# Expert stage of a gated transformer block on one core: gate and up matmuls with the weights held in the array and 128 tokens passing

## The chip, the core and the metric

The kernel runs on one core of a Trainium2 chip. The metric is device time in microseconds (us) of one launch. A core has TensorE (PE: matmuls, which read SBUF and write PSUM, and whose weight loads the trace lists apart as PEld), VectorE (DVE), ScalarE (ACT), GpSimd (POOL) and SyncE (SP, here a DMA queue). The engines run their own instruction lists in order and meet at semaphores.

## The reference

The block does `x = x + tanh(g) * attention(layernorm(x), ctx)` and then a mixture of experts on 128 sequences of 128 tokens, 256 channels. What the change touches is the second part, cut to what matters:

```
x = x + jnp.tanh(g_ffn[0]) * _L0_ffn_ref(_layernorm(x, axis=-1), w_router, w_fc, w_gate, w_proj)

cap = int(LOAD * K * max(1, T / E))        # 16 slots per expert and sequence, K = 2, E = 16
gg = jnp.einsum('enc,ech->enh', expert_inputs, w_gate)
h  = jnp.einsum('enc,ech->enh', expert_inputs, w_fc)
h  = jax.nn.silu(gg) * h                   # h: 128 hidden channels
o  = jnp.einsum('enh,ehc->enc', h, w_proj)
y  = sum over the two chosen experts of probability * o
```

## The kernel before

Three blocks follow each other: `attention_block`, `routing_block` and `expert_block`. The change lies in the last one, but for one factor in `routing_block` (L983).

**Precision.** Every matmul of the expert block is split: each operand is a head (`_hi`, rounded to fp32r) and a rest (`_lo`), and `split_matmul` (L1256) issues three fp32r matmuls, head by head, head by rest and rest by head, each with a weight load of its own. The trace names a product as `out<-moving,stationary`.

**Units.** A unit is one step of a software pipeline written by hand. Unit n means two things at once: sequence n for the sequence-wise steps, and for the expert-wise steps the pair of experts j = n mod 8 in the group of eight sequences n div 8 (16 slots of each of 8 sequences are 128 token rows). The constants of L1046 say by how many units each step runs behind or ahead of GATE. In one turn of the loop each engine does, in this order:

- PE (L1263): OUTPUT of unit u-3, that is `EO`: 2 experts x 3 matmuls, 256 columns passing. HIDDEN of u-2: two transposes `HT` of the hidden tile. GATE of u, `GU`: 2 experts x 2 halves of the channels x 3 matmuls; here the tokens (`s_hi`, `s_lo`) are the stationary operand and 256 weight columns pass (128 of the gate, 128 of fc), so that a result has tokens on the partitions. DISPATCH of u+9, `DS`: 4 matmuls of 256 columns that pick a sequence's tokens into expert slots.
- ACT (L1169): copies `EO` to SBUF (`eo`), makes `h_hi` from the transposes, issues the DMA of `eo` to DRAM, makes `x_hi`, the tanh of the gate (`th`, L1195) and `s_hi`.
- DVE (L1208): `h_lo`, `pick`, the first half of the output sum (L1228), `(tanh+1)*gate` (L1235), times fc (`hid`, L1239), the second half of the output sum (L1243), `s_lo` (L1249). Silu is thus made of tanh, and the factor 0.5 sits in `weight` (L983).
- POOL (L1146): two indirect DMAs that gather a sequence's rows of `eo_d` (`first`, `second`, L1153; their descriptors are made on POOL), and `x_lo` (L1162).
- SP (L1122): the output's DMA, the load of `xn2_d` into a ring of 3 and of `x1_d` into a ring of 3.

The steps FETCH and COLLECT (gather and output sum) start only with unit 12 and 14, since a gather needs all experts of its group. PE runs 16 units of the 128 as the body of a loop; the other engines' lists are written out. The steps before the first GATE are nine units of DISPATCH alone.

Of the kernel before, what the change touches and what calls it, by code (L numbers as in the profile page):

```python
# [858 lines left out]
def routing_block(nc, ctx, T, D):  # L859
# [82 lines left out]
    def _(dve):  # L942
# [40 lines left out]
        then(dve.tensor_scalar(weight[:], prob[:], gates[:, 3:4], 0.5, ALU.mult, ALU.mult))  # L983
# [59 lines left out]
def expert_block(nc, ctx, T, D):  # L1043


    LOAD, PICK, DISPATCH, GATE, HIDDEN, OUTPUT, FETCH, COLLECT = -13, -11, -9, 0, 2, 3, 12, 14  # L1046
# [8 lines left out]
    def pb(name):  # L1055
# [4 lines left out]
    x_in_sb, xr, y_sb = tiles[:, 0:3], tiles[:, 3:6], tiles[:, 6:8]  # L1060
    x_hi = sb("x_hi", [P, 2, DIM], F32R)
# [4 lines left out]
    th = sb("th", [P, 2, 2, HID])  # L1066
    hid = sb("hid", [P, 2, 2, HID])
# [11 lines left out]
    names = ("x_hi_done x_lo_done pick_done ds_done s_hi_done s_lo_done gu_done th_done "  # L1079
             "gated_done hid_done ht_done h_hi_done h_lo_done eo_done eo_copied y_part_done out_done").split()  # L1080
    M = {n: sem(n) for n in names}
    x_in = [sem(f"xn2_in{r}") for r in range(3)]
    rows_in = [sem(f"rows_in{r}") for r in range(3)]
    x1_in = [sem(f"x1_in{r}") for r in range(3)]
    eo_out = [sem(f"eo_out{r}") for r in range(3)]
    y_out = [sem("y_out0"), sem("y_out1")]
    DS = [pb("DS0"), pb("DS1")]
    HT = [pb("HT0"), pb("HT1")]
# [24 lines left out]
    def flat(a):  # L1113
        return a.rearrange("p a b -> p (a b)")
# [5 lines left out]
    @block.sync  # L1120
    def _(sp):
        def step(unit, on):  # L1122
            n = unit(COLLECT)
            if on(COLLECT):
                sp.wait_ge(M["out_done"], n.n + 1)
                sp.dma_start(D["out"][bass.ds(n.n, 1)].rearrange("b t c -> t b c"),
                             y_sb[:, n.slot(2):n.slot(2) + 1]).then_inc(y_out[n.slot(2)], 16)
            n = unit(LOAD)
            if on(LOAD):
                wait_for(sp, M["x_hi_done"], n.n - 2)  # L1130
                wait_for(sp, M["x_lo_done"], n.n - 2)
                sp.dma_start(x_in_sb[:, n.turn(3):n.turn(3) + 1], D["xn2_d"][:, bass.ds(n.n, 1)]) \  # L1132
                    .then_inc(x_in[n.turn(3)], 16)
            n = unit(FETCH)
            if on(FETCH):
                wait_for(sp, M["y_part_done"], n.n - 2)
                sp.dma_start(xr[:, n.turn(3):n.turn(3) + 1], D["x1_d"][:, bass.ds(n.n, 1)]) \  # L1137
                    .then_inc(x1_in[n.turn(3)], 16)

        run_flat(sp, step)  # L1140
        for q in y_out:
            sp.wait_ge(q, 16 * (SEQS // 2))

    @block.gpsimd
    def _(pool):
        def step(unit, on):  # L1146
# [21 lines left out]
    def _(act):  # L1168
        def step(unit, on):  # L1169
            n = unit(OUTPUT)  # L1170
# [4 lines left out]
            n = unit(HIDDEN)  # L1175
            if on(HIDDEN):
                act.wait_ge(M["ht_done"], n.n + 1)
                wait_for(act, M["eo_done"], n.n - 1)
                act.activation(flat(h_hi[:, n.slot(2)]), HT[n.slot(2)][:, 0:2 * P], ACT.Copy) \
                    .then_inc(M["h_hi_done"], 1)  # L1180
# [5 lines left out]
            n = unit(PICK)  # L1186
            if on(PICK):
                act.wait_ge(x_in[n.turn(3)], n.landed(3))
                wait_for(act, M["ds_done"], n.n - 1)
                act.activation(x_hi[:, n.slot(2)], x_in_sb[:, n.turn(3)], ACT.Copy).then_inc(M["x_hi_done"], 1)  # L1190
# [191 lines left out]
```

## Time and profile before

| | us |
|---|---|
| median of 3 runs | 1836.87 (1833.91 to 1838.42) |
| the profiled execution's own time | 1835.99 |
| its span on the core | 1834.2 |
| PE / PEld busy | 1520.0 / 1222.3 |
| DVE / ACT / POOL busy | 1410.9 / 1133.7 / 1088.1 |
| expert stage, from the first DS matmul (1344.28 us) to the end | 489.9 |

An instruction's duration in the trace includes its latency, so neighbours on one engine overlap: what one more matmul costs is read from the distance of starts, not from its duration. "idle before" in brackets is time in which the engine stood still before that row, and what ended it; "issue" is a release that the profile doesn't name. PEclk is the granted TensorE clock, 1.00 for 2.4 GHz and 0.50 for 1.2 GHz.

### The profile page before, as it was taken

Reading aid. Unit: us, or ns where it says so; the run is one execution under the profiler, and the core shown is the slowest. Engines: PE = TensorE matmul, PEld = TensorE weight load, DVE = VectorE, ACT = ScalarE, POOL = GpSimd, SP = SyncE. Lnnn points to the kernel's source line nnn. Section 1 sums busy time; section 2 is a strip of 40 time slices with the busy share of each in tenths; the row PEclk is TensorE's granted clock in tenths of the full one; section 3 lists DMA queues with packets and bytes.
Section 4 is the critical chain, followed back from the end, with each engine's and each line's share of the span. In section 5 each row is a group of like instructions: output and inputs, shape, how many; then the busy total and the mean of one; then the engine's idle time right before and its main releaser. Section 6 shows DMA issues by size and latency. Waiting matters only on the chain. (4 is left out here: it accounts for less than half of the span.)

```text
span 1834.2 us, 50716 instructions
## 1 busy us (share of the span) xinstructions
PE 1520.0 (83%) x16843; PEld 1222.3 (67%) x16844; DVE 1410.9 (77%) x2993; ACT 1133.7 (62%) x2321; POOL 1088.1 (59%) x1490
## 2 busy tenths in 40 slices
PE   4888889988899898898988989986169888898871
PEld 3666666666666666666666666664059888898871
DVE  3777787777877777777777777775968999999964
ACT  3667667677666766766766767674236555565540
POOL 3455465555655555555555555551826888788866
PEclk9999999999999999999999999997569999999995
DMA  2112122121221211212212122242026888898876
GB/s 90 48 58 86 57 71 72 57 86 57 69 74 57 85 58 57 86 57 73 70 57 86 57 70 73 70 145 81 6 72 198 260 263 261 262 286 269 263 228 207
DMA packets 156096, 210.21 MB, mean 115 GB/s; under 512 B 18688, under 2 KB 104832, under 8 KB 156032
## 3 DMA queue, kind: packets, MB, share of 16 engines
q1 hardware_dynamic: 125312, 142.36, 24.5%
q0 software_dynamic: 12288, 33.57, 6.4%
q10 hardware_dynamic: 18432, 33.56, 5.1%
q8 instruction: 24, 0.39, 0.1%
q14 instruction: 40, 0.33, 0.1%
HBM read 125.54 MB, written 83.89 MB: 114 GB/s over the span
## 5 line engine op out<-in xcount | busy, mean ns | idle before, releaser
L505 DVE TRANSPOSE_TENSOR_REDUCE part_max<-ST 128x16 f32<-128x512 f32 x512 | 321.3, 685 | 171.9 <-PE ST L684 168.4
L360 ACT ACTIVATE probs_t<-ST 128x512 f32<-128x512 f32 x512 | 262.5, 596 | 68.2 <-PE ST L699 68.2
L711 PE MATMUL PO<-probs_t,v_aug 128*32 128x128 f32 x4096 | 205.2, 298 | 108.6 <-ACT probs_t L360 95.0
L288 POOL TENSOR_TENSOR ct_lo<-c_in_sb,ct_hi 128x512 fp32r<-128x512 f32 x64 | 82.4, 1288 | 278.0 <-ACT ct_hi L378 278.0
L711 PEld LDWEIGHTS PO<-probs_t,v_aug 128*32 128x32 f32 x4096 | 94.4, 114 | 204.5 <-ACT probs_t L360 192.6
L437 ACT ACTIVATE xn<-x_in_sb,off,rstd 128x256 f32<-128x256 f32 x128 | 70.0, 594 | 224.7 <-POOL off L284 224.7
L1190 ACT ACTIVATE x_hi<-scaled 128x256 fp32r<-128x256 f32 x128 | 53.5, 418 | 210.9 <-DMA scaled<-xn_d 131.9
L1259 PE MATMUL GU<-we_hi,s_hi 128*128 128x256 f32 x512 | 155.8, 304 | 0.0
L1153 POOL DMA_INDIRECT first<-eo_d,collect_row x128 | 126.0, 984 | 44.4 <-issue 24.0
L316 POOL TENSOR_TENSOR q_rest<-q_rot,q_head 128x512 f32<-128x512 f32 x64 | 82.4, 1288 | 112.7 <-ACT q_head L413 112.7
L1153 POOL DMA_INDIRECT second<-eo_d,collect_row x128 | 122.6, 958 | 42.3 <-issue 38.7
L1260 PE MATMUL GU<-we_hi,s_lo 128*128 128x256 f32 x512 | 145.2, 284 | 0.0
L1261 PE MATMUL GU<-we_lo,s_hi 128*128 128x256 f32 x512 | 145.1, 283 | 0.0
L1162 POOL TENSOR_TENSOR x_lo<-scaled,x_hi 128x256 fp32r<-128x256 f32 x128 | 115.2, 900 | 48.8 <-ACT x_hi L1190 46.7
L1259 PE MATMUL EO<-we_hi,h_hi 128*128 128x256 f32 x256 | 82.5, 322 | 53.2 <-issue 39.4
L366 ACT ACTIVATE out_t<-PO 128x512 f32<-128x512 f32 x128 | 78.6, 614 | 71.0 <-PE PO L711 71.0
L729 PE MATMUL F<-ident_sb,xn 128*128 128x128 f32 x512 | 91.8, 306 | 31.6 <-ACT xn L437 19.7
L679 PE MATMUL ST<-q_hi,k_hi 32*128 32x256 f32 x1024 | 94.6, 358 | 5.9 <-issue 5.4
L1260 PEld LDWEIGHTS GU<-we_hi,s_lo 128*128 128x128 f32 x512 | 98.6, 192 | 0.0
L1261 PEld LDWEIGHTS GU<-we_lo,s_hi 128*128 128x128 f32 x512 | 98.1, 192 | 0.0
L1259 PEld LDWEIGHTS GU<-we_hi,s_hi 128*128 128x128 f32 x512 | 97.9, 191 | 0.2 <-issue 0.2
L1259 PEld LDWEIGHTS EO<-we_hi,h_hi 128*128 128x128 f32 x256 | 49.0, 191 | 72.9 <-issue 63.2
(158 smaller groups left out, 5565.7 us busy)
## 6 DMA issues: line engine op xcount, KB each, us to landing
eo_d<-eo ACTq DMA_DIRECT2D x128, 256.0 KB
x_in_sb<-x SPq DMA_DIRECT2D x64, 256.0 KB, 2.8
c_in_sb<-ctx_t SPq DMA_DIRECT2D x64, 256.0 KB, 2.8
xr_sb<-x SPq DMA_DIRECT2D x64, 256.0 KB, 4.0
x_d<-x SPq DMA_DIRECT2D x64, 256.0 KB, 4.1
xn_d<-xn SPq DMA_DIRECT2D x64, 256.0 KB, 4.2
scaled<-xn_d SPq DMA_DIRECT2D x128, 128.0 KB
scaled<-x_d SPq DMA_DIRECT2D x128, 128.0 KB
```

The source lines that it names most:

```text
L288: pool.tensor_tensor(ct_lo[:].rearrange("p k b t -> p (k b t)"), c_in_sb[:, n.par].rearrange("p k b t -> p (k b t)"), ct_hi[:].rearrange(" ...
L316: pool.tensor_tensor(q_rest[:].rearrange("p k t -> p (k t)"), q_rot[:].rearrange("p k t -> p (k t)"), q_head[:].rearrange("p k t -> p (k t ...
L360: act.activation(probs_t[:, b, i].rearrange("p j q -> p (j q)"), ST[i][:], ACT.Exp) \
L505: dve.tensor_reduce(part_max[:, i, 0], ST[i][:].rearrange("p (c l) -> p c l", l=32), AX_X, ALU.max, apply_transpose=True).then_inc(M["part ...
L679: pe.matmul(ST[i][:, m * 2 * SEQ:(m + 1) * 2 * SEQ], k_part[rows, n.par, m, b], q_part[rows, n.par, m, b].rearrange("p e t -> p (e t)"), s ...
L711: last = pe.matmul(PO[32 * j:32 * j + 32, i * SEQ:(i + 1) * SEQ], v_aug[:, n.par, b, head], probs_t[:, b, i, j], start=True, stop=True)
L729: last = pe.transpose(F[:, (2 * k + b) * SEQ:(2 * k + b + 1) * SEQ], src[:, b, k * P:(k + 1) * P], ident[:])
L1153: pool.indirect_dma_start(out=dst[:, n.turn(3)], out_offset=None, in_=D["eo_d"][n.group].rearrange("r e c -> (r e) c"), in_offset=bass.Ind ...
L1162: pool.tensor_tensor(x_lo[:, n.slot(2)], x_in_sb[:, n.turn(3)], x_hi[:, n.slot(2)].bitcast(F32), ALU.subtract).then_inc(M["x_lo_done"], 1)
L1259: pe.matmul(out, lh, rh, start=first, stop=False)
L1260: pe.matmul(out, ll, rh, start=False, stop=False)
L1261: return pe.matmul(out, lh, rl, start=False, stop=last)
```

## The change

- GU: the weights become the stationary operand, 128 columns of one expert's gate or fc at a time (`part` 0 to 3), and the 128 token slots pass. 4 parts x 2 halves x 3 = 24 matmuls of 128 columns take the place of 12 of 256. The result has the hidden channels on the partitions, as EO's stationary operand needs them, and the two transposes HT with their PSUM banks go.
- ACT computes Silu itself (`gate`), and DVE multiplies by fc in one instruction in place of two. `h_hi` and `h_lo` are made from `gate` in SBUF. The factor 0.5 in `weight` goes.
- `x_lo` moves from POOL to DVE; its ring stays 2 deep, `x_hi` becomes 4 deep and its ACT step (HEAD) runs a unit earlier, its load 3 units ahead of it.
- The output is summed in place in the ring `xr`, which becomes 4 deep, and `y_sb` goes. SP's list is turned to load, fetch, output.
- HIDDEN and OUTPUT run one unit earlier (1 and 2 behind GATE).

```diff
-        then(dve.tensor_scalar(weight[:], prob[:], gates[:, 3:4], 0.5, ALU.mult, ALU.mult))
+        then(dve.tensor_scalar(weight[:], prob[:], gates[:, 3:4], None, ALU.mult))
...
-    LOAD, PICK, DISPATCH, GATE, HIDDEN, OUTPUT, FETCH, COLLECT = -13, -11, -9, 0, 2, 3, 12, 14
+    LOAD, HEAD, PICK, DISPATCH, GATE, HIDDEN, OUTPUT, FETCH, COLLECT = -14, -11, -10, -9, 0, 1, 2, 12, 14
...
-    x_in_sb, xr, y_sb = tiles[:, 0:3], tiles[:, 3:6], tiles[:, 6:8]
-    x_hi = sb("x_hi", [P, 2, DIM], F32R)
+    x_in_sb, xr = tiles[:, 0:4], tiles[:, 4:8]
+    x_hi = sb("x_hi", [P, 4, DIM], F32R)
...
-    th = sb("th", [P, 2, 2, HID])
-    hid = sb("hid", [P, 2, 2, HID])
+    gate = sb("gate", [P, 2, 2, HID])
...
-            n = unit(PICK)
-            if on(PICK):
-                pool.wait_ge(M["x_hi_done"], n.n + 1)
-                wait_for(pool, M["ds_done"], n.n - 1)
-                pool.tensor_tensor(x_lo[:, n.slot(2)], x_in_sb[:, n.turn(3)], x_hi[:, n.slot(2)].bitcast(F32),
-                                   ALU.subtract).then_inc(M["x_lo_done"], 1)
...
+            n = unit(HIDDEN)
+            if on(HIDDEN):
+                act.wait_ge(M["hid_done"], n.n + 1)
+                wait_for(act, M["eo_done"], n.n - 1)
+                act.activation(flat(h_hi[:, n.slot(2)]), flat(gate[:, n.slot(2)]), ACT.Copy) \
+                    .then_inc(M["h_hi_done"], 1)
...
-                wait_for(act, M["hid_done"], n.n - 1)
-                act.activation(th[:, n.slot(2)], GU[n.slot(2)][:].rearrange("p (e f n) -> p e f n", e=2, f=2)[:, :, 0],
-                               ACT.Tanh, scale=0.5).then_inc(M["th_done"], 1)
+                wait_for(act, M["h_lo_done"], n.n - 1)
+                act.activation(gate[:, n.slot(2)], GU[n.slot(2)][:].rearrange("p (e f n) -> p e f n", e=2, f=2)[:, :, 0],
+                               ACT.Silu).then_inc(M["gate_done"], 1)
...
             n = unit(PICK)
             if on(PICK):
+                dve.wait_ge(M["x_hi_done"], n.n + 1)
                 wait_for(dve, M["ds_done"], n.n - 1)
+                dve.tensor_tensor(x_lo[:, n.slot(2)], x_in_sb[:, n.turn(4)], x_hi[:, n.turn(4)].bitcast(F32),
+                                  ALU.subtract).then_inc(M["x_lo_done"], 1)
...
+            n = unit(GATE)
+            if on(GATE):
+                gu = GU[n.slot(2)][:].rearrange("p (e f n) -> p e f n", e=2, f=2)
+                dve.wait_ge(M["gate_done"], n.n + 1)
+                dve.tensor_tensor(gate[:, n.slot(2)], gate[:, n.slot(2)], gu[:, :, 1], ALU.mult).then_inc(M["hid_done"], 1)
...
-                dve.scalar_tensor_tensor(out=th[:, n.slot(2)], in0=th[:, n.slot(2)], scalar=1.0, in1=gu[:, :, 0],
-                                         op0=ALU.add, op1=ALU.mult).then_inc(M["gated_done"], 1)
...
-                for e in range(2):
-                    last = pe.transpose(HT[n.slot(2)][:, e * P:(e + 1) * P], hid[:, n.slot(2), e], ident[:])
-                last.then_inc(M["ht_done"], 1)
...
-                for e in range(2):
-                    at = n.j * (4 * HID) + e * 2 * HID
+                for part in range(4):
+                    at = n.j * (4 * HID) + part * HID
                     for k in range(KC):
-                        last = split_matmul(GU[n.slot(2)][:, e * 2 * HID:(e + 1) * 2 * HID],
-                                            [t[:, n.side, k, n.j * 2 + e].rearrange("p b s -> p (b s)")
-                                             for t in (s_hi, s_lo)],
-                                            [w[:, k, at:at + 2 * HID] for w in w_gu], k == 0, k == KC - 1)
+                        last = split_matmul(GU[n.slot(2)][:, part * P:(part + 1) * P],
+                                            [w[:, k, at:at + HID] for w in w_gu],
+                                            [t[:, n.side, k, n.j * 2 + part // 2].rearrange("p b s -> p (b s)")
+                                             for t in (s_hi, s_lo)], k == 0, k == KC - 1)
```

Two engines' lists show the move. PE, in the loop body, from the end of one unit's EO into its GU, before:

```order
L1261 MATMUL EO<-we_lo,h_hi 128x256
L1280 MATMUL HT<-ident,hid 128x128 x2
L1259 MATMUL GU<-we_hi,s_hi 128x256
L1260 MATMUL GU<-we_hi,s_lo 128x256
L1261 MATMUL GU<-we_lo,s_hi 128x256
```

and in the change (the helper `split_matmul` has moved to L1249 to L1251):

```order
L1250 MATMUL EO<-we_hi,h_lo 128x256
L1251 MATMUL EO<-we_lo,h_hi 128x256
L1249 MATMUL GU<-s_hi,we_hi 128x128
L1250 MATMUL GU<-s_hi,we_lo 128x128
L1251 MATMUL GU<-s_lo,we_hi 128x128
```

The transposes are gone, and the group of three GU rows, which stood four times in a unit, stands eight times, each row half as wide.

DVE, one whole unit in the middle of the stage, before:

```order
L1213 TENSOR_TENSOR h_lo<-HT,h_hi 128x256
L1218 TENSOR_TENSOR pick<-logits,iota_sb 128x256
L1228 SCALAR_TENSOR_TENSOR scaled<-first,weight,scaled 128x256
L1235 SCALAR_TENSOR_TENSOR th<-th,GU 128x256
L1239 TENSOR_TENSOR hid<-th,GU 128x256
L1243 SCALAR_TENSOR_TENSOR scaled<-second,weight,scaled 128x256
L1249 TENSOR_TENSOR s_lo<-DS,s_hi 128x32x16
```

and in the change:

```order
L1205 TENSOR_TENSOR h_lo<-gate,h_hi 128x256
L1211 TENSOR_TENSOR x_lo<-scaled,x_hi 128x256
L1213 TENSOR_TENSOR pick<-logits,iota_sb 128x256
L1222 TENSOR_TENSOR gate<-gate,GU 128x256
L1227 SCALAR_TENSOR_TENSOR scaled<-first,weight,scaled 128x256
L1233 TENSOR_TENSOR s_lo<-DS,s_hi 128x32x16
L1238 SCALAR_TENSOR_TENSOR scaled<-second,weight,scaled 128x256
```

DVE keeps seven instructions in a unit: `x_lo` has come, one of the two gate instructions has gone, and the second half of the output sum stands last.

## Rows read from the trace of the kernel before

**Rows 1.** The page: span, busy time of each engine

```profile
span 1834.2 us, 50716 instructions
PE 1520.0 (83%) x16843; PEld 1222.3 (67%) x16844; DVE 1410.9 (77%) x2993; ACT 1133.7 (62%) x2321; POOL 1088.1 (59%) x1490
```

**Rows 2.** Busy time by stretch (columns: us, engines' busy us, PEclk, DMA share, GB/s)

```profile
1369.00:1397.00 28.00, 28.00 (x233) 27.80 (x233) 21.30 (x49) 19.27 (x50) 9.58 (x12) 1.00 0.40 136
1403.00:1567.00 164.00, 143.61 (x1122) 135.45 (x1122) 151.29 (x329) 92.41 (x234) 135.79 (x141) 1.00 0.84 262
1795.00:1834.00 39.00, 5.29 (x22) 4.25 (x21) 15.35 (x33) 2.34 (x5) 25.45 (x26) 0.50 0.69 209
```

**Rows 3.** Timeline of POOL, one round (start us, us, engine line op, tiles)

```profile
1506.09 0.96 POOL L1153 DMA_INDIRECT first<-eo_d,collect_row  x1 [0.18 <-issue]
1507.36 0.95 POOL L1153 DMA_INDIRECT second<-eo_d,collect_row  x1 [0.30 <-issue]
1508.33 0.99 POOL L1162 TENSOR_TENSOR x_lo<-scaled,x_hi 128x256 fp32r<-128x256 f32 x1
1509.50 0.97 POOL L1153 DMA_INDIRECT first<-eo_d,collect_row  x1 [0.18 <-issue]
```

**Rows 4.** Timeline of DVE in the same round

```profile
1505.84 0.41 DVE L1213 TENSOR_TENSOR h_lo<-HT,h_hi 128x256 fp32r<-128x256 f32 x1
1506.17 0.41 DVE L1218 TENSOR_TENSOR pick<-logits,iota_sb 128x256 fp32r<-128x256 f32 x1
1506.93 0.41 DVE L1235 SCALAR_TENSOR_TENSOR th<-th,GU 128x256 f32<-128x256 f32 x1
1507.71 1.01 DVE L1243 SCALAR_TENSOR_TENSOR scaled<-second,weight,scaled 128x256 f32<-128x256 f32 x1
```

**Rows 5.** Timelines of PE and of PEld in the same round

```profile
1506.35 0.35 PE L1259 MATMUL EO<-we_hi,h_hi 128*128 128x256 f32 x1 [0.34 <-issue]
1507.47 0.28 PE L1260 MATMUL GU<-we_hi,s_lo 128*128 128x256 f32 x1
1507.59 0.28 PE L1261 MATMUL GU<-we_lo,s_hi 128*128 128x256 f32 x1
...
1507.48 0.19 PEld L1261 LDWEIGHTS GU<-we_lo,s_hi 128*128 128x128 f32 x1
...
1508.66 0.28 PE L1261 MATMUL GU<-we_lo,s_hi 128*128 128x256 f32 x1
1509.76 0.35 PE L1259 MATMUL EO<-we_hi,h_hi 128*128 128x256 f32 x1 [0.34 <-issue]
```

**Rows 6.** Timeline of PEld at the transposes, early in the expert stage

```profile
1372.41 0.24 PEld L1280 LDWEIGHTS HT<-ident,hid 128*128 128x128 f32 x2
1372.62 0.19 PEld L1259 LDWEIGHTS GU<-we_hi,s_hi 128*128 128x128 f32 x1
```

**Rows 7.** Timeline of PE, first EO matmul of two units running, same place

```profile
1371.73 0.35 PE L1259 MATMUL EO<-we_hi,h_hi 128*128 128x256 f32 x1
1374.63 0.30 PE L1259 MATMUL EO<-we_hi,h_hi 128*128 128x256 f32 x1
```

**Rows 8.** Timeline of PE at the lower clock, end of the stage

```profile
1794.93 0.41 PE L1260 MATMUL EO<-we_hi,h_lo 128*128 128x256 f32 x1
1795.78 0.41 PE L1261 MATMUL EO<-we_lo,h_hi 128*128 128x256 f32 x1
```

**Rows 9.** Timeline of PE: first GU matmul, next unit, last GU

```profile
1357.68 0.55 PE L1259 MATMUL GU<-we_hi,s_hi 128*128 128x256 f32 x1
1361.07 0.28 PE L1259 MATMUL GU<-we_hi,s_hi 128*128 128x256 f32 x1
1791.37 0.28 PE L1261 MATMUL GU<-we_lo,s_hi 128*128 128x256 f32 x1
```

**Rows 10.** Timeline of PE: the router's plain fp32 matmuls in the attention stage

```profile
605.71 0.63 PE L763 MATMUL F<-x2t,wr 128*32 128x128 f32 x8
```

**Rows 11.** Timeline of ACT: its table load

```profile
0.74 1.28 ACT L351 ACT_TABLE_LOAD   x1 [0.74 <-PEq L1376]
```

More of the change, by code:

```diff
@@ L1122, in step @@
         def step(unit, on):
+            n = unit(LOAD)
+            if on(LOAD):
+                wait_for(sp, M["x_hi_done"], n.n - 3)
+                wait_for(sp, M["x_lo_done"], n.n - 3)
+                sp.dma_start(x_in_sb[:, n.turn(4):n.turn(4) + 1], D["xn2_d"][:, bass.ds(n.n, 1)]) \
+                    .then_inc(x_in[n.turn(4)], 16)
+            n = unit(FETCH)
+            if on(FETCH):
+                wait_for(sp, y_out[n.turn(4)], (n - 4).landed(4))
+                sp.dma_start(xr[:, n.turn(4):n.turn(4) + 1], D["x1_d"][:, bass.ds(n.n, 1)]) \
+                    .then_inc(x1_in[n.turn(4)], 16)
             n = unit(COLLECT)
@@ L1126, in step @@
                 sp.dma_start(D["out"][bass.ds(n.n, 1)].rearrange("b t c -> t b c"),
[L1127 to L1138, printed above, removed]
+                             xr[:, n.turn(4):n.turn(4) + 1]).then_inc(y_out[n.turn(4)], 16)
         run_flat(sp, step)
-        for q in y_out:
-            sp.wait_ge(q, 16 * (SEQS // 2))
+        for r, q in enumerate(y_out):
+            sp.wait_ge(q, 16 * len(range(r, SEQS, 4)))
     @block.gpsimd
@@ L1185, in step @@
                     .then_inc(eo_out[n.turn(3)], 16)
[L1186 to L1190, printed above, removed]
+            n = unit(HEAD)
+            if on(HEAD):
+                act.wait_ge(x_in[n.turn(4)], n.landed(4))
+                wait_for(act, M["ds_done"], n.n - 3)
+                act.activation(x_hi[:, n.turn(4)], x_in_sb[:, n.turn(4)], ACT.Copy).then_inc(M["x_hi_done"], 1)
             n = unit(GATE)
@@ L1212, in step @@
                 wait_for(dve, M["eo_done"], n.n - 1)
-                dve.tensor_tensor(flat(h_lo[:, n.slot(2)]), HT[n.slot(2)][:, 0:2 * P],
+                dve.tensor_tensor(flat(h_lo[:, n.slot(2)]), flat(gate[:, n.slot(2)]),
                                   flat(h_hi[:, n.slot(2)]).bitcast(F32), ALU.subtract).then_inc(M["h_lo_done"], 1)
@@ L1225, in step @@
                 dve.wait_ge(rows_in[n.turn(3)], n.landed(3, 32))
[L1226 to L1229 removed]
+                dve.wait_ge(x1_in[n.turn(4)], n.landed(4))
+                dve.scalar_tensor_tensor(out=xr[:, n.turn(4)], in0=first[:, n.turn(3)],
+                                         scalar=weight[:, 0, bass.ds(n.n, 1)], in1=xr[:, n.turn(4)],
                                          op0=ALU.mult, op1=ALU.add).then_inc(M["y_part_done"], 1)
[L1231 to L1245 removed]
             n = unit(DISPATCH)
@@ L1250, in step @@
                                   tokens(s_hi, n).bitcast(F32), ALU.subtract).then_inc(M["s_lo_done"], 1)
+            n = unit(COLLECT)
+            if on(COLLECT):
+                dve.wait_ge(M["y_part_done"], n.n + 1)
+                dve.scalar_tensor_tensor(out=xr[:, n.turn(4)], in0=second[:, n.turn(3)],
+                                         scalar=weight[:, 1, bass.ds(n.n, 1)], in1=xr[:, n.turn(4)],
+                                         op0=ALU.mult, op1=ALU.add).then_inc(M["out_done"], 1)
         run_flat(dve, step)
@@ L1300, in step @@
                 wait_for(pe, M["s_lo_done"], n.n - 1)
+                slot = n.slot(4)
                 for k in range(KC):
                     out = DS[n.slot(2)][:, k * SLOTS:(k + 1) * SLOTS]
-                    pe.matmul(out, x_hi[:, n.slot(2), k * P:(k + 1) * P], pick[:, n.slot(2)], start=True, stop=False)
+                    pe.matmul(out, x_hi[:, slot, k * P:(k + 1) * P], pick[:, n.slot(2)], start=True, stop=False)
                     last = pe.matmul(out, x_lo[:, n.slot(2), k * P:(k + 1) * P], pick[:, n.slot(2)],
```

38 lines of the change are left out of this document (5 added, 33 removed).

## The prediction

> **What bounds the kernel now.** I read the page first: in 1834.2 us PE is busy 83%, DVE 77%, POOL 59% [rows 1]. These are means over three stages. The change lies in the last one, so I read busy time by stretch [rows 2]. The expert stage has two phases. From 1369 to 1397 us, before any gather has started, PE is busy 28.00 of 28.00 us: PE sets the pace. The first EO matmuls of two units running are 2.90 us apart [rows 7]. From 1403 on the output is collected too; PE is busy 143.61 of 164, DVE 151.29, and a unit takes 1509.76 - 1506.35 = 3.41 us [rows 5]. There POOL's list runs without a break: gather, gather, `x_lo`, gather, from 1506.09 to 1509.50, 3.41 us again [rows 3]. While POOL runs `x_lo` (0.99 us), DVE's second output sum, which overlaps it, takes 1.01 us, against 0.41 for other instructions of 128x256 [rows 4]. So POOL and DVE hold each other up there, and PE stands idle 0.34 us before EO [rows 5]. Most of the 128 units run like this; in others `x_lo` is shorter and a unit somewhat shorter too.
>
> **What a pair on PE costs.** Every matmul here has its own weight load. Over ten distances, from 1507.47 to 1508.66, starts of GU matmuls lie 0.119 us apart; a load begins together with the matmul before its own (1507.48 and 1507.47), and its matmul starts when 0.11 to 0.12 us have gone (1507.59) [rows 5]. Which of the two sets the distance, the load of 128 columns or the passing of 256? At the lower clock (1.2 GHz) four distances of the same pair take 1795.78 - 1794.93 = 0.85 us, 0.213 each [rows 8]. That is 256 columns at 1.2 GHz with nothing left over. At 2.4 GHz passing alone would be half, 0.107; the trace shows 0.119. Something that doesn't halve sets the upper clock's distance by a hair, and the load is what is left. Two rows agree: two transposes, each a load of 128 columns with only 128 passing, advance the loads by 1372.62 - 1372.41 = 0.21 us, 0.105 each [rows 6]; passing alone would be 0.053. So a pair whose moving side is halved should keep nearly its price.
>
> **The change part by part.** Let p be the price of a pair with 128 columns passing.
>
> GU: 12 pairs of 0.119 go, 1.43 us a unit; 24 pairs come, 24p. With p = 0.119 that is 2.86, so +1.43. HT: two pairs of 0.105 go, and the longer step to the first GU matmul behind them, some 0.08 (2.90 less 22 x 0.119 and 0.21): -0.29. PE per unit is then 24p + 10 x 0.119 = 24p + 1.19, 4.05 us, against 3.41 for POOL and DVE today. PE becomes the bound throughout, and what lies on the other engines is cover:
>
> - POOL loses `x_lo`, 0.99 us a unit, and with it DVE's stretched sum loses up to 0.6. Neither is worth anything if PE needs 4.05.
> - DVE gets `x_lo` (by `pick`, two sources of the same shape, 0.41 and a distance of about 0.35) and loses `th<-th,GU`, 0.41 [rows 4]: nothing. If PE did not cover it, this would stay even.
> - ACT: Silu for tanh, same shape, one instruction for one. A second table load comes once; the one in the trace took 1.28 us [rows 11]. It lies before the first gate result: 0 to 1.3 us, I take 0.
> - EO one unit earlier: `h_lo` of a unit is then due one PE unit after its GU. Silu, product, head and rest are four instructions of at most 0.41 us each, 1.6 us in a row, and PE has DS, EO and the next GU between, over 4 us. Hidden.
> - Rings of 4 and SP's new order: a load has more time, never less. The output DMA now stands behind a load that may wait, but with PE at 4.05 us nothing on SP is late.
> - The factor 0.5 sits in one instruction on DVE before the stage; nothing.
>
> **The sum**, on the profiled execution's clock. First GU matmul at 1357.68, unchanged [rows 9]. Two units have no EO: 28 pairs each, 24p + 0.48; the first begins at the lower clock, and took 3.39 us for 16 pairs [rows 9] where 16 x 0.119 = 1.90, so 1.49 more. Then 126 units of 24p + 1.19. The last nine have no DS: -9 x 0.48 = -4.3. From the end of the last GU matmul, 1791.37 + 0.28, to 1834.2 are 42.6 us, POOL's 26 last gathers above all [rows 2, 9]; they stay (some 5 us less is possible, as collecting would no longer lag). The execution's own time, 1835.99, is 1.8 us above its span. Together 1550.2 + 3072p. For p = 0.119: 1915.8, I say **1916 us**, against 1836 for this execution and a median of 1836.87, so 4.3% slower. The formula also gives where it turns: at p = 0.093 it reaches today's time.
>
> **p from both sides.** The row nearest is the fp32r pair itself at 0.119, as load and types are the same and only the passing is halved; I take it. Transposes give 0.105: 1873 us. Allowing 0.125: 1934. So the likeliest case alone is 1868 to 1936. The trace's farthest ends are 0.053 (passing alone, a quarter of 0.213) and the router's fp32 matmuls of 128 columns, below.
>
> The Trainium skill ("TensorE: Matmul & The Clock Gate", section on LDWEIGHTS) makes a load the number of columns over 1.2 GHz, 107 ns for 128, whatever the rows. By that rule p is 0.107 and the sum 1879; the trace shows 0.119 for a pair whose passing needs less, so I keep the row.
>
> **Rivals.**
>
> *Load hidden, time falls (15%).* If successive loads overlap and the 0.012 us over passing are something else, p is 0.053 to 0.093 and PE needs 2.5 to 3.4 us a unit. Then the freed POOL and DVE count. What decides next is data: the DMA engines are busy 0.84 of the time at 3.41 us a unit [rows 2], 2.87 us of work, so a unit can't go far under 3.0. Some 116 collecting units gain 0.4 and twelve early ones 0.3: 1836 - 50 = 1786 at best. For it: the two freed engines are the bound today. Against: the transposes' 0.105. It decides from p below 0.093.
> The same page, section "Back-to-back issue gap", has about 81 ns for a sustained pair with 128 columns; by it PE would need 3.13 us and the sum would be 1799. No row here shows fp32r with 128 columns.
>
> *Load and passing in a row (10%).* A load starts with the matmul before its own; if a short matmul can't cover it and they go one after the other, p = 0.119 + 0.053 = 0.172: 2079 us. Against: the transposes would show it, and don't.
>
> *Narrow fp32r at the price of full fp32 (14%).* No fp32r matmul in this trace passes fewer than 256 columns, so that the fast rate holds for 128 is not shown. The router's four fp32 matmuls of 128 columns are 8 rows in 0.63 us [rows 10]: less the 0.28 of the last, 0.05 a row, two column groups side by side, two rows a matmul, so 0.20; four passes of 0.053 are 0.213. The sum is 2165 to 2205 us.
>
> *The clock falls (4%).* The array passes columns less than half of the time. At 1.2 GHz the ten wide pairs cost 2.13, the 24 narrow ones 0.119 to 0.213: 5.0 to 7.2 us a unit, around 2190 in the middle. Against: in the attention stage PE also issues many 128-column rows, such as [rows 10].
>
> *No change that can be told (2%)*: p happens to be near 0.093.
>
> **The numbers.** The forecast has 55%. The cases of slower time together have 83%, faster 15%, within 0.3% (5.5 us, about what a measurement of this kernel can tell) 2%. The range must hold 8 in 10: the forecast's own from 1868, and up to the full price of fp32, 2205, so 1868 to 2210; the faster rivals are left out, and part of the clock's.
>
> **What would show it.** In the changed profile, starts of GU rows 0.119 us apart, PE busy nearly all of the collecting phase with no idle before EO, units of 4.05 us from the first to the last, 24 GU loads a unit, POOL idle over a third, DVE's second sum at 0.5 us. GU distances under 0.093, or PE still waiting, would make the forecast wrong; 0.17 or 0.2 would leave its direction and break its size; PEclk at 0.5 would name the clock.

## The result, and the profile after

The changed kernel takes 1903.2 us (median of four runs, 1893.55 to 1910.28) against 1835.39 for the kernel before on the same chip: 1.0364 times as long, interval 1.0302 to 1.0426. A second measurement on another chip (`after_again` below) gave 1.0357, 1.0333 to 1.0381. The prediction was 1916, 4.3% slower; it came out 3.6% slower. The profiled execution took 1893.55 us, with a span of 1891.8.

The page of the changed kernel, span and busy time of each engine; these lines answer to [rows 1]:

```profile
span 1891.8 us, 52896 instructions
...
PE 1627.6 (86%) x18124; PEld 1349.3 (71%) x18124; DVE 1370.9 (72%) x2993; ACT 1161.8 (61%) x2322; POOL 977.0 (52%) x1362
```

PE gained 108 us of busy time and became the only engine over 75%. DVE and POOL lost some. Busy time by stretch (engines' busy us, granted clock, DMA share, GB/s), which answers to [rows 2]:

```profile
1369.00:1397.00 28.00, 28.00 (x244) 28.00 (x244) 14.69 (x36) 15.70 (x36) 0.00 (x0) 0.99 0.31 100
1403.00:1567.00 164.00, 164.00 (x1439) 164.00 (x1439) 116.59 (x288) 92.99 (x212) 79.24 (x80) 1.00 0.73 229
```

While output is collected, PE is busy 164 of 164 us where it had 143.61, and its loads fill the stretch as well. DVE falls from 151.29 to 116.59. Even the DMA engines have less to do per us, 0.73 for 0.84, because everything runs at PE's pace. POOL, whose figure stands last of the five, has 79.24, under half.

The timeline of PE in that stretch (start us, us, line, tiles), against [rows 5]:

```profile
1503.78 0.33 PE L1287 MATMUL DS<-pick,x_hi 128*128 128x256 f32 x1
...
1504.31 0.28 PE L1249 MATMUL EO<-we_hi,h_hi 128*128 128x256 f32 x1
...
1505.03 0.22 PE L1249 MATMUL GU<-s_hi,we_hi 128*128 128x128 f32 x1
1505.09 0.28 PE L1250 MATMUL GU<-s_hi,we_lo 128*128 128x128 f32 x1
1505.21 0.27 PE L1251 MATMUL GU<-s_lo,we_hi 128*128 128x128 f32 x1
1505.32 0.27 PE L1249 MATMUL GU<-s_hi,we_hi 128*128 128x128 f32 x1
1505.43 0.27 PE L1250 MATMUL GU<-s_hi,we_lo 128*128 128x128 f32 x1
...
1506.43 0.27 PE L1250 MATMUL GU<-s_hi,we_lo 128*128 128x128 f32 x1
```

There is no idle time before EO any more. From 1505.21 to 1506.43 lie eleven distances, 1.22 us, 0.111 each. The duration of a row, 0.27, is pipelined and says nothing on the pace; only the distance does. The EO rows stay 0.12 apart. The next unit's first EO stands 3.88 us later (1508.19), and so in every unit from the second on, as long as DS runs; the last nine units, without DS, take 3.40. It is a list that never waits.

Who waits now, from 1400 to 1850 us (total us, times, longest):

```profile
POOL first L1151 <- DVE scaled L1238: 181.8, 109, 13.6
ACT gate L1187 <- PE GU L1251: 132.8, 117, 2.0
DVE gate L1222 <- ACT gate L1187: 130.4, 117, 1.7
```

These are the longest, and PE is not among those that wait: the other three wait for PE, or for one another behind it. ACT stands over 1 us a unit before the GU results.

And DVE's second output sum, which took 1.01 us beside POOL's `x_lo` [rows 4]:

```profile
1505.75 0.48 DVE L1238 SCALAR_TENSOR_TENSOR scaled<-second,weight,scaled 128x256 f32<-128x256 f32 x1
1506.14 0.42 DVE L1205 TENSOR_TENSOR h_lo<-gate,h_hi 128x256 fp32r<-128x256 f32 x1
```

So the change did free DVE and POOL, and it paid for that with PE time that was not there.

At the start of the stage the clock tells more. Timeline of PE at the lower clock:

```profile
1355.67 0.41 PE L1250 MATMUL GU<-s_hi,we_lo 128*128 128x128 f32 x1
1355.88 0.41 PE L1251 MATMUL GU<-s_lo,we_hi 128*128 128x128 f32 x1
1356.10 0.41 PE L1249 MATMUL GU<-s_hi,we_hi 128*128 128x128 f32 x1
...
1357.38 0.41 PE L1249 MATMUL GU<-s_hi,we_hi 128*128 128x128 f32 x1
```

Eight distances take 1.71 us, 0.214 each, with 128 columns passing. That is the price which the wide pair has at this clock in [rows 8]. And the clock stayed low for longer than before:

```profile
1360.00:1366.00 6.00, 6.00 (x30) 6.00 (x29) 2.12 (x5) 1.59 (x4) 0.00 (x0) 0.50 0.07 22
1366.00:1368.00 2.00, 2.00 (x11) 2.00 (x11) 0.42 (x1) 0.64 (x2) 0.00 (x0) 0.50 0.00 0
1368.00:1370.00 2.00, 2.00 (x13) 2.00 (x12) 1.62 (x4) 1.25 (x3) 0.00 (x0) 0.56 0.00 0
1370.00:1374.00 4.00, 4.00 (x38) 4.00 (x36) 1.26 (x4) 2.19 (x5) 0.00 (x0) 1.00 0.34 100
```

PE works without a break, and is granted 0.50 (1.2 GHz) until about 1369.7, then 1.00 (2.4 GHz).

### The profile page after: what moved, and what is told of

It reads as the page before. It is cut to its first block and busy times, and to the rows that moved or that the text cites. A ratio compares the mean times of both kernels' runs of the same rounds, so it can differ in the third digit from the quotient of the medians.

```text
span 1891.8 us, 52896 instructions
## 1 busy us (share of the span) xinstructions
PE 1627.6 (86%) x18124; PEld 1349.3 (71%) x18124; DVE 1370.9 (72%) x2993; ACT 1161.8 (61%) x2322; POOL 977.0 (52%) x1362
## 5 line engine op out<-in xcount | busy, mean ns | idle before, releaser
L1250 PE MATMUL GU<-s_hi,we_lo 128*128 128x128 f32 x1024 | 284.5, 278 | 0.0
L1251 PE MATMUL GU<-s_lo,we_hi 128*128 128x128 f32 x1024 | 283.6, 277 | 0.0
L1249 PE MATMUL GU<-s_hi,we_hi 128*128 128x128 f32 x1024 | 276.7, 270 | 0.0
L1151 POOL DMA_INDIRECT first<-eo_d,collect_row x128 | 132.7, 1037 | 263.4 <-DVE scaled L1238 185.4
L1249 PEld LDWEIGHTS GU<-s_hi,we_hi 128*128 128x128 f32 x1024 | 199.1, 194 | 0.0
L1250 PEld LDWEIGHTS GU<-s_hi,we_lo 128*128 128x128 f32 x1024 | 199.1, 194 | 0.0
L1251 PEld LDWEIGHTS GU<-s_lo,we_hi 128*128 128x128 f32 x1024 | 199.1, 194 | 0.0
L1222 DVE TENSOR_TENSOR gate<-gate,GU 128x256 f32<-128x256 f32 x128 | 53.9, 421 | 151.4 <-ACT gate L1187 151.4
L1187 ACT ACTIVATE gate<-GU 128x256 f32<-128x256 f32 x128 | 49.4, 386 | 150.2 <-PE GU L1251 150.2
L729 PEld LDWEIGHTS F<-ident_sb,xn 128*128 128x128 f32 x512 | 58.2, 149 | 58.0 <-issue 52.8
```

Of the source, the lines that this page charges most:

```text
L729: last = pe.transpose(F[:, (2 * k + b) * SEQ:(2 * k + b + 1) * SEQ], src[:, b, k * P:(k + 1) * P], ident[:])
L1151: pool.indirect_dma_start(out=dst[:, n.turn(3)], out_offset=None, in_=D["eo_d"][n.group].rearrange("r e c -> (r e) c"), in_offset=bass.Ind ...
L1249: pe.matmul(out, lh, rh, start=first, stop=False)
L1250: pe.matmul(out, ll, rh, start=False, stop=False)
L1251: return pe.matmul(out, lh, rl, start=False, stop=last)
```

## The experiments

Two questions were asked. The first: what sets the price of a narrow pair, and is PE alone the loss? The second: what is the other half of the change worth, and why didn't it pay? n64, w64, n256 and before_narrow were each executed once, beside 1838.95 us for the kernel before; their readings rest on distances in the trace. The diffs below show only the lines that matter.

### 1. n64: half as many columns pass

```diff
-    GU[n.slot(2)][:, part * P:(part + 1) * P]     ... t[...].rearrange("p b s -> p (b s)")
+    GU[n.slot(2)][:, part * P:part * P + P // 2]  ... t[...].rearrange("p b s -> p (b s)")[:, 0:P // 2]
```

> The changed kernel with only 64 of the 128 token columns passing in each GU matmul; the weights in the array are unchanged, 128 columns (the other half of the tokens is left out: its hidden values are stale). Load theory (the load of 128 weight columns sets the pair): GU pairs stay 0.111 to 0.112 us apart at the upper clock, units stay 3.88 us, time 1893 to 1910 us as the change. Passing theory (a narrow fp32r matmul passes at two clocks a column): pairs fall to about 0.056 us, PE needs 2.5 us a unit, another engine or the data binds at about 3.0, time near 1790 us. Floor theory (every fp32r matmul takes 256 clocks, whatever its shape): 0.111 us, as the load theory.

The diff leaves out, here and in w64, four matmuls that fill the GU banks once before the stage. Measured: 2313.6 us. The timeline of PE:

```profile
1503.18 0.40 PE L1250 MATMUL GU<-s_hi,we_lo 128*128 128x64 f32 x1
1503.39 0.40 PE L1251 MATMUL GU<-s_lo,we_hi 128*128 128x64 f32 x1
```

That of its weight loads:

```profile
1503.11 0.33 PEld L1250 LDWEIGHTS GU<-s_hi,we_lo 128*128 128x128 f32 x1
1503.32 0.33 PEld L1251 LDWEIGHTS GU<-s_lo,we_hi 128*128 128x128 f32 x1
```

And the stretch by busy time, clock and DMA:

```profile
1403.00:1567.00 164.00, 164.00 (x771) 164.00 (x770) 60.51 (x145) 52.86 (x115) 34.25 (x35) 0.50 0.36 106
```

The granted clock was 1.00 from 1342.7 to 1349.5 us, before any narrow matmul, and 0.50 from there to the end, with PE busy throughout. That is the rival in which the clock falls, but in a kernel other than the changed one. The expectation, 1893 to 1910 us, missed this by 400 us. The distance is 0.21 us with 64, 128 (the changed kernel, above) and 256 columns passing [rows 8], at the same clock. So what passes is not what sets it with 64 and 128 columns. What all three share is the load of 128 columns. A fixed price of every matmul (the expectation's floor theory) would look the same; the next run tells the two apart.

### 2. w64: half as many columns loaded

```diff
-    GU[n.slot(2)][:, part * P:(part + 1) * P]            ... w[:, k, at:at + HID]
+    GU[n.slot(2)][0:P // 2, part * P:(part + 1) * P]     ... w[:, k, at:at + HID // 2]
```

> The changed kernel with only 64 of the 128 weight columns in the array for each GU matmul, 128 token columns passing (half of the hidden channels is left out). Load theory: the load halves, pairs fall to 0.056 to 0.07 us, PE is no longer the bound, a unit takes about 3.0 us, time near 1790 us. Passing theory and floor theory: pairs stay 0.111 us, 3.88 us a unit, 1893 to 1910 us.

Measured: 1923.6 us. The timeline of PE:

```profile
1506.36 0.22 PE L1251 MATMUL GU<-s_lo,we_hi 128*64 128x128 f32 x1
1506.42 0.22 PE L1249 MATMUL GU<-s_hi,we_hi 128*64 128x128 f32 x1
1506.48 0.22 PE L1250 MATMUL GU<-s_hi,we_lo 128*64 128x128 f32 x1
...
1507.17 0.22 PE L1249 MATMUL GU<-s_hi,we_hi 128*64 128x128 f32 x1
1508.34 0.22 PE L1250 MATMUL GU<-s_hi,we_lo 128*64 128x128 f32 x1 [0.94 <-issue]
```

The pair costs 0.060 us where it cost 0.111, with the same 128 columns passing: **the load sets the price of the narrow pair.** What a load of 64 columns costs by itself isn't shown, only that it is at most 0.060, since 128 passing columns need 0.053 (an estimate, a quarter of the 0.213 of [rows 8]). Yet the time didn't follow. Units of 2.7 us alternate with units of 4 to 6: PE stops inside a GU group with no semaphore to wait for (0.94 us, "issue"), its granted clock is 0.89 from 1403 to 1567 us, and ACT stands before `gate` for 54.8 us in 18 waits with a releaser that the profile can't name. The same kind of ACT wait returns in experiment 5. PE's own stops in this kernel were not traced to a cause.

### 3. n256: 24 matmuls again, but 256 columns pass

```diff
-    GU[...][:, part * P:(part + 1) * P]                            ... n.j * 2 + part // 2
+    GU[...][:, (part // 2) * 2 * P:(part // 2 + 1) * 2 * P]        ... n.j * 2:n.j * 2 + 2
```

> The changed kernel with 256 token columns passing in each of the 24 GU matmuls (the tokens of both experts through each expert's weights, so the hidden values are not the reference's). Load theory: passing twice the columns costs almost nothing, a pair goes from 0.111 to the 0.119 us of the other wide pairs, a unit from 3.88 to 4.05 to 4.07 us, time about 1915 us. If narrow columns were passed at a slower rate than wide ones, the result is the same here; if passing and loading added up, a pair would take about 0.165 us and the time would be above 2050 us. Also read here: when the clock rises at the start of the stage, with wide instead of narrow matmuls.

Measured: 1913.3 us, units of 4.08 us. The timeline of PE:

```profile
1505.22 0.28 PE L1249 MATMUL GU<-s_hi,we_hi 128*128 128x256 f32 x1
1505.34 0.28 PE L1250 MATMUL GU<-s_hi,we_lo 128*128 128x256 f32 x1
```

Doubling what passes costs 0.008 us a pair (0.12 for 0.111). This unit is what the prediction had put down for the changed kernel (4.05), since its p was taken from such a pair. The clock rose sooner: from 1358 it is 1.00, where the changed kernel had 0.50 to nearly 1370. That gave back part of the difference.

### 4. before_narrow: the kernel before with GU in 24 narrow matmuls

```diff
-    for e in range(2):
-        split_matmul(GU[...][:, e * 2 * HID:(e + 1) * 2 * HID], s_hi/s_lo, w[:, k, at:at + 2 * HID])
+    for part in range(4):
+        split_matmul(GU[...][:, part * HID:(part + 1) * HID], s_hi/s_lo, w[:, k, at:at + HID])
```

> The kernel before with one thing changed: each GU matmul of 256 weight columns is cut into two of 128, the tokens stay in the array and are loaded twice (24 pairs in place of 12, same results, transposes kept). Load theory: the price of 24 narrow pairs does not depend on which operand is loaded: PE needs 24 x 0.112 + 1.19 + 0.29 = 4.17 us a unit, time about 1930 us, more than the change itself. If the price in the change came from the weights' tiles (their address or layout) the pairs here would be 0.06 to 0.09 us and the time about 1836 us.

Measured: 1927.8 us, pairs 0.11 apart, units of 4.09 us, PE busy 164.00 of 164. Nothing of the change is in it but twice the number of GU pairs, each half as wide, and it is 89 us over the kernel before. Which operand sits in the array makes no difference (0.11 us either way); the count of loads does. The rest of the change took back some 25 us of this, and PE's own list accounts for all of it: without the transposes a unit takes 3.88 us in place of 4.09, 27 us over 128 units.

### 5 and 6. wide_rest and wide_pool: the rest of the change without its narrow matmuls

wide_rest has the wide GU, the transposes and the lags of before, with everything else of the change: `x_lo` on DVE, Silu, rings of 4, the output added in place. wide_pool is the same with `x_lo` back on POOL.

```diff
-    for part in range(4):  split_matmul(GU[...], w, s)      # the change
+    for e in range(2):     split_matmul(GU[...], s, w)      # as before
+    pe.transpose(HT[...], gate[:, n.slot(2), e], ident[:])
```

> The changed kernel with only the GU part taken back: 12 matmuls of 256 weight columns with the tokens in the array, the two transposes HT and the lags 2 and 3 of before; Silu on ScalarE, x_lo on VectorE, the rings of 4 and SP's order stay. If the 24 loads are the whole loss and the other edits are a gain that they covered: PE needs 2.91 us a unit, POOL 2.5, VectorE about 2.9, the DMA engines 2.87 us of work, so a unit takes 3.0 to 3.1 us and the time is 1785 to 1800 us, below both kernels. Rival: the moved x_lo makes VectorE the bound, or a loop of waits through ScalarE and VectorE holds a unit at 3.4 us or more: 1830 us or above.

> wide_rest with x_lo back on POOL, so that beside the kernel before only Silu, the saved VectorE instruction, the rings and SP's order differ. If POOL's list (two gathers and x_lo, 3.41 us) and its overlap with VectorE's second sum were the bound of the kernel before: units stay 3.2 to 3.4 us, time 1815 to 1836 us. If VectorE's seven instructions were the bound and the saved one is what counts: units fall by 0.3 to 0.4 us, 1790 to 1800 us, as wide_rest.

Measured: wide_rest 1853.9 us, 1.0079 times the kernel before (1.0063 to 1.0096); wide_pool 1843.9, 1.0021 (1.0007 to 1.0036). So with PE relieved and POOL and DVE freed, wide_rest was 0.8% *slower* than before, against an expectation of 1785 to 1800. wide_pool lies outside both of its ranges. There the longest waits of PE's list are for POOL, from 1403 to 1567 us:

```profile
PE DS L1298 <- POOL x_lo L1161: 19.3, 39, 1.5
```

The stage, wide_rest:

```profile
1403.00:1567.00 164.00, 136.44 (x1102) 133.12 (x1102) 127.67 (x317) 98.44 (x226) 88.92 (x90) 0.99 0.81 252
```

No engine is full: PE 136, DVE 128, ACT 98, POOL 89 of 164. Before any gather, units took 2.85 us, PE's own time. Afterwards 45 `eo` writes are issued in 164 us, 3.64 a unit (the expectation of the next runs says 3.44; that was read too low). One or two units of 2.9 us and a long one of some 4.6 us take turns. The timeline of ACT at a long one:

```profile
1505.29 0.60 ACT L1167 ACTIVATE eo<-EO 128x512 f32<-128x512 f32 x1 [0.65 <-PE EO L1252]
1506.01 0.38 ACT L1172 ACTIVATE h_hi<-HT 128x256 fp32r<-128x256 f32 x1
1506.02 0.35 ACTq L1177 DMA_DIRECT2D eo_d<-eo  x1
1506.47 0.42 ACT L1183 ACTIVATE x_hi<-scaled 128x256 fp32r<-128x256 f32 x1
1508.99 0.38 ACT L1188 ACTIVATE gate<-GU 128x256 f32<-128x256 f32 x1 [2.10 <-remote]
```

The last GU row before it, and the EO behind it:

```profile
1506.00 0.28 PE L1252 MATMUL GU<-we_lo,s_hi 128*128 128x256 f32 x1
1511.89 0.36 PE L1250 MATMUL EO<-we_hi,h_hi 128*128 128x256 f32 x1 [1.86 <-ACT h_hi L1172]
```

By its row GU, for which `gate` waits, was complete at 1506.28. `gate` starts at 1508.99, 2.10 us after `x_hi`, and the view names no releaser ("remote"). The product on DVE, the transposes and `h_hi` queue up behind it, and PE pays: its next EO waits 1.86 us for `h_hi`. Two things stand close to each such wait: the issue of the 256 KB write of `eo` in ACT's own queue two instructions earlier, and DMA engines that are 0.81 busy. The next two runs take one of them away each.

The trace's semaphore records tell more than the view. The signal by which the last GU matmul releases `gate` is recorded at 1508.96, 2.68 us after that row's end, and `gate` starts 0.02 us behind it. The signals of DS, EO and HT come late with it, all between 1509.71 and 1509.84. So ACT was not standing at its DMA issue: it had run `x_hi` behind it, and then waited for a signal of PE that came late. From 1403 to 1567 us 36 of 45 GU signals are recorded more than 0.06 us after their row's end, the latest by 3.4 us; in w64 it is 20 of 39, up to 3.8 us. Why they are late stays open. The ends of PE's rows are modelled, so PE may have run later than its rows say, or the signals may have been held; and of some 726 semaphore records that this stretch should have, 440 are there.

### 7. after_again

> The changed kernel itself again, for its spread: of four executions two took 1893 to 1896 us with a mean granted clock of 0.938 and two 1910 us at 0.930. If the 15 us are a longer stretch at the lower clock at the start of the expert stage (there a pair takes 0.213 instead of 0.111 us, so 0.102 us are lost on each): every execution near 1910 us has the lower mean clock, and a profile of one shows PEclk at 0.50 for some 30 us longer, with the units after it at 3.88 us as ever. If they are something else (data, gathers), the clock is the same and units are longer throughout.

Measured: 1902.6 us (1899.76 to 1912.9), 1.0357 (1.0333 to 1.0381) on the chip of wide_rest and wide_pool. The changed kernel is 49 us over wide_rest, which differs from it in GU and what hangs on it alone.

Over all ten executions the mean granted clock falls as the time grows, but for 0.001: 0.938 at 1893.6 us, 0.935 at 1900.4, 0.930 at 1910.3, 0.928 at 1912.9. So the spread goes with the clock, as the first reading said. Where the clock was lost in an execution near 1910 us isn't shown, since none was profiled. In the profiled one here (1899.76 us, a span 4.6 us longer than the first's) it was not the start of the stage, where the clock again rose at 1369.7: all units are as long as in the first profile but the last two, 4.98 and 6.43 us instead of 3.40. There ACT waited once more with no named releaser, and from 1851.0 us on the clock is 0.50, 7 us before the last GU matmul ends (timelines of ACT and of PE):

```profile
1849.48 0.38 ACT L1187 ACTIVATE gate<-GU 128x256 f32<-128x256 f32 x1 [4.21 <-remote]
1851.67 0.55 PE L1249 MATMUL EO<-we_hi,h_hi 128*128 128x256 f32 x1 [1.41 <-ACT h_hi L1166]
```

### 8 and 9. wide_less and wide_spq: fewer bytes, or another queue

```diff
 wide_less (SP)
-    sp.dma_start(xr[...], D["x1_d"][:, bass.ds(n.n, 1)])
+    if n.n < 4: sp.dma_start(xr[...], D["x1_d"][:, bass.ds(n.n, 1)])
 wide_spq
-    act.wait_ge(M["eo_copied"], n.n + 1); act.dma_start(D["eo_d"]..., eo[...])
+    sp.wait_ge(M["eo_copied"], n.n + 1);  sp.dma_start(D["eo_d"]..., eo[...])    (ahead of the write of out)
```

> wide_rest took 1853.9 us in units of 2.85, 2.85 and 4.57 us (mean 3.44), although no engine was busy for 3.44 us of one; its DMA engines were busy for 0.81 of the stage (2.78 us of a unit). This run is wide_rest without the loads of x1 after the fourth: a later sequence's output adds to what the ring's buffer holds from an earlier one, so the output is not the reference's; 124 of 128 loads of 128 KB are left out, one seventh of the unit's 896 KB, and a DVE wait on x1 becomes one on the output of four units earlier. Theory A (the DMA engines' traffic is what the unit of 3.44 us waits for): the mean unit falls by about a seventh towards 2.95 to 3.05 us, the long units become rarer, and the time 1800 to 1812 us, below the kernel before. Theory B (the stall is ACT's own, from the order of its queue): the long unit stays every second to third time and the time within 8 us of 1854. In both DVE and POOL have as much to do as before.

> wide_rest with the same traffic, but the write of eo is issued from SP's queue, ahead of the write of out, instead of from ACT's queue. Theory A (DMA traffic): same bytes, same mean unit of 3.4 us, 1846 to 1862 us. Theory B (ACT is held behind its own DMA issue, since all of its stalls of 2.1 us stand one or two instructions behind it): the stalls before ACT's gate go, the unit falls to 2.9 to 3.1 us and the time to 1795 to 1815 us.

Measured, beside 1835.22 for the kernel before: wide_less 1762.8 us, 0.9600 (0.9575 to 0.9626); wide_spq **1789.4 us, 0.9743 (0.9713 to 0.9772)**. Each theory said of one of the runs that it would not help, and both did. The stretch in wide_less:

```profile
1403.00:1567.00 164.00, 163.17 (x1373) 162.92 (x1372) 160.27 (x401) 129.82 (x286) 112.72 (x113) 1.00 0.88 273
```

The same in wide_spq:

```profile
1403.00:1567.00 164.00, 156.44 (x1288) 153.70 (x1287) 148.50 (x375) 115.45 (x268) 104.63 (x106) 1.00 0.94 298
```

In wide_spq a unit moves the same bytes as in wide_rest, and the DMA engines carry 298 GB/s where they carried 252. So the traffic was no bound in wide_rest; theory A, as put, is wrong. Who waited from 1403 to 1567 us, in wide_rest:

```profile
ACT gate L1188 <- remote: 24.6, 12, 2.2
```

And in wide_spq:

```profile
ACT gate L1188 <- PE GU L1252: 25.6, 54, 0.5
POOL first L1157 <- DMA eo_d<-eo: 29.3, 29, 3.2
DVE scaled L1228 <- DMA second<-eo_d,collect_row: 14.7, 18, 1.7
```

Twelve waits of 2 us with no name are gone, and 54 of 0.5 us for the GU results, which are PE's pace, stand in their place. All 53 GU signals of the stretch are recorded within 0.06 us of their row's end. What is left are waits for DMA, on POOL and on DVE: with engines 0.94 busy, data seem to be what a unit meets now. 53 `eo` writes in 164 us are 3.09 us a unit, of which 2.90 us the DMA engines work.

But wide_less keeps the write in ACT's queue and has no long wait either (its longest before `gate` is 0.2 us, and all 57 GU signals are prompt), at 2.86 us a unit and PE busy 163 of 164. So in this kernel the late signals need both: the write in ACT's queue, and the full traffic. Taking away either removes them. wide_spq leaves nothing of the computation out, and is faster than both kernels.

Theory B had the right remedy, but its mechanism, ACT held behind its own issue, is not what the semaphore records show. How the write's queue delays PE's signals stays open, and one rival is untested: in wide_spq the write is also issued later, behind SP's two loads, 3.1 us after its data are copied (median) instead of 0.03, so the moment of issue may matter and not the queue. The other traces fit the two conditions. Of the nine with the write in ACT's queue and full traffic, seven have ACT waits of this kind in the expert stage, though most of them only one to three; of the five with the write in SP's queue or less traffic, none has.

The Trainium skill ("DMA: Bandwidth & Descriptors", section "Issuing engines are not separate DMA queues") says that issuing from several engines "will only save the time on the sequencer", usually small. By that rule the move should be worth little. The issue row in the timeline above is short, 0.35 us, and the move was worth 3.3% all the same. So in this kernel it saved more than the time of the issue; in the two kernels of the next section, which wait for something else, it saved next to nothing, as the rule has it.

### 10 and 11. after_spq and before_spq: the same move in the two kernels

> The changed kernel with the write of eo issued from SP's queue, as in wide_spq; nothing else is touched. PE is the bound of the changed kernel and its units of 3.88 us leave ACT and DVE room, so a stall of ACT of 2 us a few times over is covered: 1898 to 1908 us, units still 3.88 us. If the ACT queue had its part in the loss of 3.6%, the time falls by more than 10 us.

> The kernel before with the write of eo issued from SP's queue. If POOL's 3.41 us a unit are the bound of the kernel before, only the units that are longer than that can shorten: 1825 to 1837 us, and the 2.6% of wide_spq need the freed POOL and DVE as well as the moved write. If instead the moved write alone gives what wide_spq gave, it comes to 1785 to 1800 us. If the later issue (SP stands ahead of it for the loads) delays the gathers, it is slower than 1840.

Measured, beside 1835.32: after_spq 1898.9 us, 1.0332 (1.0297 to 1.0367), units of 3.88 us; before_spq 1836.9, 1.0007 (0.999 to 1.0023). PE bounds the one and, for most of the stage, POOL with DVE the other, and neither gains clear of its interval by the queue (the changed kernel had 1.0364 and 1.0357 with the write on ACT). The gain of wide_spq therefore needs both halves, the freed engines and the moved write, and is not the move alone.

### 12. before_less: the kernel before with a seventh less traffic

```diff
-    sp.dma_start(xr[...], D["x1_d"][:, bass.ds(n.n, 1)])
+    if n.n < 3: sp.dma_start(xr[...], D["x1_d"][:, bass.ds(n.n, 1)])
```

> The kernel before without the loads of x1 after the third (so a later sequence's output adds to a stale buffer and is not the reference's), the same seventh of the traffic as in wide_less. If POOL's 3.41 us a unit are what bounds the kernel before, as the prediction read it, the time stays within 6 us of its 1837. If the DMA traffic shares that bound, it falls by more than 8 us, at most to the 3.41 us units of POOL without any longer one, about 1820.

Measured: 1814.2 us, 0.9879 (0.9854 to 0.9905): 21 us less than before, more than the reading "POOL alone" allows, and below the 1820 of its floor. The group of POOL's `x_lo` from 1403 to 1567 us in the kernel before:

```profile
L1162 POOL TENSOR_TENSOR x_lo<-scaled,x_hi 128x256 fp32r<-128x256 f32 x47 | 46.2, 983 | 0.9
```

In before_less:

```profile
L1162 POOL TENSOR_TENSOR x_lo<-scaled,x_hi 128x256 fp32r<-128x256 f32 x50 | 43.7, 874 | 0.9
```

`x_lo` takes 0.99 us beside DVE's output sum and about 0.74 otherwise. Without the loads the short form is more frequent in this stretch, 24 of 49 rounds instead of 4 of 46, and such a round takes 3.14 us, not 3.41. But from 1403 to 1703 us it is only 33 of 89 instead of 28 of 86. Counted by EO, units 12 to 60 took 8.9 us less than before, the next 54 only 1.0, and the last 13 took 11.8 us less. In the kernel before, ACT and PE stand still in those last units (timelines of ACT and of PE):

```profile
1763.08 0.60 ACT L1201 ACTIVATE s_hi<-DS 128x512 fp32r<-128x512 f32 x1 [2.48 <-remote]
1766.01 0.60 ACT L1174 ACTIVATE eo<-EO 128x512 f32<-128x512 f32 x1 [2.34 <-remote]
1767.44 0.55 PE L1259 MATMUL EO<-we_hi,h_hi 128*128 128x256 f32 x1 [4.42 <-ACT h_hi L1179]
```

These are the waits of wide_rest again, and before_less has none. So the 3.41 us of [rows 3] are no fixed sum: the two engines' lists can stand in a better or a worse place to each other. That data which come sooner shift them is a guess; more than half of the 21 us came from elsewhere.

## Why the prediction was right, and where it wasn't

- **The direction, and PE as the bound: right.** The changed profile has PE busy in all of the collecting phase, no idle before EO, POOL idle for half, the second sum at 0.48 us, equal units to the end. before_narrow shows that the doubled loads alone cost 89 us.
- **p, "I take it", 0.119: a little too high.** The narrow pair costs 0.111 to 0.112: a unit of 3.88 less 1.19 leaves 24 x 0.112. In the formula that is 3072 x 0.007, 22 us too much. The step chose the wide pair as the nearest row, although its 256 passing columns need 0.107 by themselves; n256 shows that they do add 0.008. The transposes at 0.105 were the bound from below, and the truth lies between the two. The Trainium skill's 107 ns for a load of 128 columns ("TensorE: Matmul & The Clock Gate", section on LDWEIGHTS) gave 1879 and was as near as the row at the upper clock. The Trainium skill's 81 ns for a sustained pair (same title, section "Back-to-back issue gap") was reached by no fp32r pair with 128 columns loaded; the least here is 0.111 us.
- **"Something that doesn't halve": wrong as reasoning, right in its conclusion.** The prediction took the load for the part that keeps its price when the clock doubles. It does not: with 128 columns passing the distance is 0.214 at 1.2 GHz and 0.111 at 2.4. Load and passing of 256 columns happen to cost the same at the lower clock, and the one row could not tell them apart. n64 and w64 did: with 128 columns passing or fewer, the load of 128 sets it.
- **The start of the stage: two small terms.** The first GU stands at 1355.56, 2.1 us earlier than before, as unit positions at the stage's start vary by some us from kernel to kernel. The stretch at the lower clock was put down with 1.49 us; the first two units took 5.97 us each instead of 4.83 and 3.34, and the next lost another 1 us, together 4.8 more. With the measured pair the upper clock would have given 3.17, 3.17 and 3.88, so the low clock cost 6.6 in all, 5.1 beyond the 1.49. The prediction let the clock rise as in [rows 9]; it rose 9 us later.
- **The tail, 42.6 us: 38.6.** The text allowed up to 5 us less, since collecting would no longer lag; 4.0 of them came.
- **The sum.** In spans: 1914.0 predicted; -21.5 for p, +5.1 for the clock, -2.1 for the start, -4.0 for the tail give 1891.5; measured 1891.8. So against the execution whose clock the sum followed the miss is 22 us. That the median is only 13 us away is partly luck: half of the executions are longer for a reason that the sum has no term for.
- **The rivals.** Serial load and passing (0.172) and the full fp32 price (0.2) did not occur. The clock did not fall, but n64 shows that it can stay low: with 64 columns passing it was 0.50 to the end. The rival "load hidden" put 1786 us on a kernel in which the freed engines count. The first test of its price, wide_rest, gave 1853.9 and seemed to refute it; what stood in the way was something that the prediction had no term for, ACT waiting for late signals of PE. With the write moved these waits went and the time was 1789.4. The collecting units gained the 0.4 us that the rival gave them; the early ones, set by PE at 2.85 for 2.90 us, did not gain its 0.3. Its sentence that "a unit can't go far under 3.0" for the DMA engines held with full traffic: 3.09.
- **The freed engines, not "worth anything if PE needs 4.05": right.** With PE relieved and the write moved, the whole is worth 2.6%.
- **What bounds the kernel before: in part.** The prediction let POOL and DVE alone set the unit while output is collected. before_less, with their work untouched, is 21 us faster, so traffic has a share in it.

## What to carry to other kernels

Count weight loads before counting columns: turning the operands of a matmul to save transposes doubled the loads of the largest group here, and 12 more of them at 0.11 us outweighed all that was freed on the other engines. When engines are freed and the time doesn't move, look for one that stands with no named releaser, and look up in the trace when the signal it waits for was recorded; then try the large DMAs from another queue. Here that was worth 3.3% in one kernel and nothing in two others. And a pair's price read at one clock can't tell load from passing when both are equal: vary one of them.

## What was not expected of the hardware

- What a weight load of 128 fp32r columns sets as the distance of matmuls scales with TensorE's clock: 0.21 us at 1.2 GHz, 0.111 at 2.4. With 64 columns loaded the distance was 0.060 at 2.4.
- PE was busy without a break for 900 us at a granted clock of 0.50 (n64). In the changed kernel the clock rose at 1369.7, with PE unbroken from 1354.5 on; in n256 it was 0.92 already from 1356 to 1358. Why the three differ isn't shown. The changed kernel's executions lie between 1894 and 1913 us, and the longer ones have the lower mean clock (0.928 against 0.938).
- With a 256 KB write a unit in ACT's queue and DMA engines 0.81 busy, 36 of 45 signals of PE to ACT were recorded late, by up to 3.4 us (wide_rest); with the write in SP's queue, or a seventh less traffic, none was, and 298 (wide_spq) and 273 (wide_less) instead of 252 GB/s moved.
